# Tail phase: gate products as four column tiles and a summing product, with a new order of work in all queues

## What is computed

```python
x = x + _L0_xattn_ref(_layernorm(x), ctx_1024, ctx_1024, Wq, ... bo)     # softmax attention, 16 heads
x = x + _L0_ffn_ref(_layernorm(x), Wc, bc, W1, b1, W2, b2)               # experts, top token per expert and set
x = x + _L1_xattn_ref(_layernorm(x), ctx_1024, ctx_1024, igate_..., fgate_...)
x = x + _L1_ffn_ref(_layernorm(x), W1, b1, W2, b2)                        # two quantized products with gelu between
```

```python
x = jnp.concatenate([q, k, v], axis=-1)          # q: the normalized x; k and v: the context
ig = x @ igate_kernel + igate_bias               # 1536 -> 8
fg = x @ fgate_kernel + fgate_bias               # 1536 -> 8
```

## Time and profile before

| | us |
|---|---|
| three runs | 2282.11, 2287.96, 2287.25 (median 2287.25) |
| the profiled execution | 2278.25 |
| its span, first to last instruction | 2276.5 |
| the tail, from 1468 us to the end | 808.5 |
| PE busy in the tail | 623.6 |

### The profile page before, as it was taken

How to read it: one execution, slowest core, us unless ns; L and a number is a source line. 1 busy time by engine, 2 the same in 40 slices (tenths; PEclk the granted TensorE clock), 3 DMA queues, 4 the chain that set the end, 5 groups by cost and what they waited for, 6 DMA issues and landing times. The chain is left out here.

```text
span 2276.5 us, 41219 instructions
## 1 busy us (share of the span) xinstructions
PE 1933.3 (85%) x14429; PEld 1218.1 (54%) x14467; DVE 1358.2 (60%) x2542; ACT 1223.8 (54%) x2239; POOL 666.9 (29%) x1205
## 2 busy tenths in 40 slices
PE   6999999999999999998496596336699899889875
PEld 3666666666666666665294294114355455446432
DVE  2757666675767667566233333314687786776763
ACT  2666556565665666555022222244776776676853
POOL 1423321322422231240030130003455345345530
PEclk9999999999999999999697697567898998988988
DMA  6424534243443533341547857686536336324200
GB/s 200 137 81 116 149 98 142 73 130 109 134 129 93 154 80 111 82 114 66 135 142 224 254 151 220 249 335 227 167 102 195 113 102 199 114 96 158 66 19 19
DMA packets 201110, 312.43 MB, mean 137 GB/s; under 512 B 30784, under 2 KB 99488, under 8 KB 193632
## 3 DMA queue, kind: packets, MB, share of 16 engines
q1 hardware_dynamic: 141936, 223.49, 31.2%
q10 hardware_dynamic: 42608, 52.97, 7.4%
q0 software_dynamic: 16384, 33.59, 5.7%
HBM read 171.30 MB, written 71.53 MB: 107 GB/s over the span
## 5 line engine op out<-in xcount | busy, mean ns | idle before, releaser
L506 DVE TENSOR_REDUCE a_negmax<-a_score 128x1 f32<-128x512 f32 x512 | 346.1, 684 | 117.2 <-PE a_score L621 109.0
L441 ACT ACTIVATE a_prob<-a_score,a_negmax 128x512 f32<-128x512 f32 x512 | 353.8, 693 | 94.9 <-DVE a_negmax L506 94.0
L317 POOL DMA_DIRECT2D a_q_stack<-a_q_parts x512 | 250.7, 498 | 520.1 <-DVE a_q_parts L500 254.1
L621 PE MATMUL a_score<-a_k_stack,a_q_stack 128*128 128x512 f32 x512 | 354.3, 692 | 9.6 <-ACT a_prob L441 7.8
L629 PEld LDWEIGHTS a_turn<-a_ident,a_prob 128*128 128x128 f32 x2048 | 254.0, 141 | 134.4 <-issue 93.2
L629 PE MATMUL a_turn<-a_ident,a_prob 128*128 128x128 f32 x2048 | 309.1, 274 | 3.4 <-ACT a_perm L417 2.0
L325 ACT COPY a_probT<-a_turn 128x512 f32<-128x512 f32 x256 | 150.0, 586 | 285.7 <-PE a_turn L629 284.0
L325 DVE COPY a_probT<-a_turn 128x512 f32<-128x512 f32 x256 | 176.3, 689 | 212.9 <-PE a_turn L629 212.6
L1943 PE MATMUL c_ff<-c_w2T,c_hqT 128*128 128x512 bf16 x482 | 140.8, 451 | 40.1 <-ACT c_hqT L1479 34.2
L621 PEld LDWEIGHTS a_score<-a_k_stack,a_q_stack 128*128 128x128 f32 x512 | 97.3, 190 | 112.4 <-issue 75.0
L890 PE MATMUL b_work<-b_blocks,b_xn 128*128 128x256 f32 x512 | 128.5, 417 | 24.7 <-POOL b_blocks L862 24.1
(11 more groups left out here) (206 smaller groups left out, 3326.0 us busy)
## 6 DMA issues: line engine op xcount, KB each, us to landing
a_k_stack<-a_k_parts SPq DMA_DIRECT2D x512, 64.0 KB, 2.6
a_q_stack<-a_q_parts POOLq DMA_DIRECT2D x512, 64.0 KB, 2.3
scratch_res<-b_res SPq DMA_DIRECT2D x32, 1024.0 KB, 5.0
c_res<-scratch_res SPq DMA_DIRECT2D x32, 1024.0 KB, 7.6
b_xn<-scratch_xn SPq DMA_DIRECT2D x68, 256.0 KB, 2.7
c_hid<-in_L_ffn_W ACTq DMA_DIRECT2D x16, 1024.0 KB, 8.4
c_negm<-scratch_m SPq DMA_DIRECT2D x64, 256.0 KB, 4.4
a_xs<-in_x ACTq DMA_DIRECT2D x8, 1024.0 KB, 5.2
```

Source lines behind the costliest of these rows:

```text
L317: eng.dma_start(stack[kind][i * DH0:(i + 1) * DH0, M % 2, g, :].bitcast(F32), parts[kind][g * DH0:(g + 1) * DH0, part, :].bitcast(F32)).th ...
L441: nc.scalar.activation(prob[:, U % 4, :], score.bank(U)[:, :], ACT.Exp, bias=negmax[:, u:u + 1], accum_out=sums[:, head_of(U), tile_of(U): ...
L506: nc.vector.tensor_reduce(negmax[:, U % UNITS:U % UNITS + 1], score.bank(U)[:, :], AX.X, ALU.max, negate=True).then_inc(max_ready, 1)
L621: nc.tensor.matmul(score.bank(U)[:, :], stack["Q"][:, M % 2, g, t * P:(t + 1) * P], stack["K"][:, M % 2, g, :], start=True, stop=True).the ...
```

## The change

The eight gate products of a batch are no longer added up in one bank. A new step GP writes four partial sums beside each other, each in its own 32 columns of the array and its own 32 partitions of one bank: quarter 0 adds products 0 and 1 of gk with xT, quarter 1 products 2 and 3, quarters 2 and 3 do the same for gkv with cT. A new ACT step GC copies the bank (128 x 512, fp32) to gate_parts. The step G is now one product of a constant matrix `picks` (128 x 40) with gate_parts: it adds the four quarters and puts the gates at the rows where they were. The weights lie in 32 columns instead of 40, with the forget gates at 8 to 15. POOL fills picks once, at the start, with a memset and 8 copies. G's bank and what reads it are as before.

All five lists are new. GP stands before DN 1 and G after it. UP 2 and UP 3 stand elsewhere: UP 2 before XT, and UP 3 before SC 0; SC 1 stands after DN 2. Of the later half: ST 1 moves up, SC 2 and SC 3 stand before MIX 0. On SP the second half of the round now reads MOUT, Y 0, GOUT, M 0, GBC 0, Y 1, GBC 1, Y 2, Y 3, X, RES 2, RES 3, M 1, M 2, GBC 2, M 3, RES 0, GBC 3, CT; the first X now comes before RES 2. On POOL: KS 0, KS 1, XG 0, XG 1, MASK 0, MASK 1, KS 2, KS 3, MASK 2, MASK 3, XG 2, XG 3. On ACT: LN 0 after SQ, RH 1 before XTC, and GELU 2 before CH 1.

```diff
-    PE_ORDER = (("UP", 1, -2), ("ST", 1, -1), ("SCO", 1, -1), ("MIX", 0, -1), ("ST", 2, -1), ("SC", 2, 0),
...
+    PE_ORDER = (("HT", 3, -2), ("W", 6, -1), ("ROWS", 0, 0), ("DN", 3, -2), ("W", 1, 0), ("XQ", 0, -1), ("W", 7, -1),
+                ("ST", 0, 0), ("W", 2, 0), ("ST", 1, 0), ("UP", 0, -1), ("UP", 1, -1), ("SCO", 0, 0), ("SC", 2, 1),
+                ("SC", 3, 1), ("TOTAL", 0, 1), ("SCO", 1, 0), ("ST", 2, 0), ("MIX", 0, 0), ("SCO", 2, 0),
+                ("MIX", 1, 0), ("SCO", 3, 0), ("ST", 3, 0), ("MIX", 2, 0), ("HT", 0, -1), ("MIX", 3, 0),
+                ("DN", 0, -1), ("UP", 2, -1), ("W", 3, 0), ("XT", 0, 1), ("HT", 1, -1), ("W", 4, 0), ("GP", 0, 1),
+                ("DN", 1, -1), ("G", 0, 1), ("W", 0, 1), ("W", 5, 0), ("UP", 3, -1), ("SC", 0, 2), ("HT", 2, -1),
+                ("DN", 2, -1), ("SC", 1, 2))
...
+                 ("SQ", 0, 0), ("LN", 0, 1), ("RH", 1, -1), ("WCOPY", 3, 0), ("XTC", 0, 1), ("SUM", 1, 4),
+                 ("SUM", 0, 5), ("QUANT", 0, 1), ("QUANT", 5, 0), ("GELU", 2, -1), ("SUM", 3, 3), ("CH", 1, -1),
+                 ("GC", 0, 1))
...
-        gk, gkv = sb("gk", [P, 3 * C, GM]), sb("gkv", [P, C, GM])
+        gk, gkv = sb("gk", [P, 3 * C, FG]), sb("gkv", [P, C, FG])
+        picks, gate_parts = sb("picks", [P, GM]), sb("gate_parts", [P, S])
...
+                nc.gpsimd.memset(picks[:, :], 0.0).then_inc(picks_ready, 1)
+                pool.wait_ge(picks_ready, 1)
+                pool.wait_ge(const, 2)
+                for j in range(C):
+                    r = slice(j * FG, (j + 1) * FG)
+                    for k in range(2):
+                        nc.gpsimd.tensor_copy(picks[r, k * FG:k * FG + H1], ident[r, j * FG + k * H1:j * FG + (k + 1) * H1]).then_inc(picks_ready, 1)
...
+                def copy_parts(m):
+                    if m > 0:
+                        wait_full(act, "G", m - 1, 0)
+                    j = job["GP", m, 0]
+                    work.wait_full(act, 0, j)
+                    nc.scalar.copy(gate_parts[:, :], work.bank(j)[:, :]).then_inc(work.free[j % 3], 1)
+                    work.wait_read(act, 0, j)
+                    act.sem_inc(parts_ready, 1)
...
-                def gates(m):
-
-                    j = job["G", m, 0]
+                def gate_products(m):
+
+                    j = job["GP", m, 0]
                     pe.wait_ge(xT_ready, (m + 1) * C)
                     pe.wait_ge(cT_in, m * 16 + 16)
                     pe.sem_inc(pe_parted, 1)
                     work.wait_free(pe, 0, j)
                     bank = work.bank(j)
-                    for c in range(C):
-                        nc.tensor.matmul(bank[0:GM, :], gk[:, c, :], xT[:, c, :], start=c == 0, stop=False)
-                    for c in range(C):
-                        last = nc.tensor.matmul(bank[0:GM, :], gkv[:, c, :], cT[:, c, :], start=False, stop=c == C - 1)
+                    for c in range(2):
+                        for q in range(C):
+                            weights, of = (gk, xT) if q < 2 else (gkv, cT)
+                            k = q % 2 * 2 + c
+                            last = nc.tensor.matmul(bank[q * FG:(q + 1) * FG, :], weights[:, k, :], of[:, k, :],
+                                                    start=c == 0, stop=c == 1, skip_group_check=True)
                     last.then_inc(work.full[j % 3], 1)
+
+                def gates(m):
+
+                    j = job["G", m, 0]
+                    pe.wait_ge(parts_ready, m + 1)
+                    work.wait_free(pe, 0, j)
+                    nc.tensor.matmul(work.bank(j)[0:GM, :], picks[:, :], gate_parts[:, :], start=True, stop=True).then_inc(work.full[j % 3], 1)
```

More of the change, by code:

```diff
@@ new lines, in tail_phase @@
+    DVE_ORDER = (("FINISH", 1, -2), ("CLIP", 5, -1), ("EXPAND", 3, -2), ("CLIP", 6, -1), ("SHIFT", 1, -1),
+                 ("ROWS", 0, 0), ("HSCALE", 3, -2), ("CLIP", 1, 0), ("FINISH", 2, -2), ("TOKENS", 0, -1),
+                 ("CLIP", 2, 0), ("COLS", 0, 0), ("CLIP", 7, -1), ("FINISH", 3, -2), ("STATE", 0, 0),
+                 ("STATE", 1, 0), ("EXPAND", 0, -1), ("EXPAND", 1, -1), ("ADD", 0, 1), ("ADD", 1, 1), ("PROD", 0, 0),
+                 ("ADD", 2, 1), ("ADD", 3, 1), ("PROD", 1, 0), ("HSCALE", 0, -1), ("STATE", 2, 0), ("PROD", 2, 0),
+                 ("MOM", 0, 1), ("PROD", 3, 0), ("STATE", 3, 0), ("CLIP", 3, 0), ("HSCALE", 1, -1), ("CLIP", 4, 0),
+                 ("SHIFT", 0, 1), ("NORM", 0, 0), ("WSCALE", 0, 1), ("FINISH", 0, -1), ("EXPAND", 2, -1),
+                 ("SCALE", 0, 0), ("HSCALE", 2, -1), ("X3", 0, 0), ("CLIP", 0, 1))
@@ new lines, in tail_phase @@
+    ACT_ORDER = (("WCOPY", 4, -1), ("RH", 2, -2), ("QUANT", 6, -1), ("LOGS", 0, 0), ("QUANT", 1, 0), ("GELU", 3, -2),
+                 ("CH", 2, -2), ("WCOPY", 0, 0), ("QUANT", 7, -1), ("SUM", 4, 2), ("LN", 1, -1), ("WCOPY", 5, -1),
+                 ("WCOPY", 6, -1), ("LATER", 0, 0), ("LOADW", 0, 10), ("QUANT", 2, 0), ("SUM", 6, 1), ("RH", 3, -2),
+                 ("CH", 3, -2), ("SUM", 7, 1), ("RT", 0, -1), ("SUM", 5, 2), ("WCOPY", 1, 0), ("CTOK", 0, -1),
+                 ("WCOPY", 7, -1), ("DEC", 0, 0), ("GELU", 0, -1), ("DEC", 1, 0), ("WCOPY", 2, 0), ("SUM", 2, 3),
+                 ("GELU", 1, -1), ("QUANT", 3, 0), ("POUT", 0, 0), ("DEC", 2, 0), ("FLOOR", 0, 0), ("POUT", 1, 0),
+                 ("DEC", 3, 0), ("RH", 0, -1), ("QUANT", 4, 0), ("POUT", 2, 0), ("CH", 0, -1), ("POUT", 3, 0),
+                 ("SQ", 0, 0), ("LN", 0, 1), ("RH", 1, -1), ("WCOPY", 3, 0), ("XTC", 0, 1), ("SUM", 1, 4),
+                 ("SUM", 0, 5), ("QUANT", 0, 1), ("QUANT", 5, 0), ("GELU", 2, -1), ("SUM", 3, 3), ("CH", 1, -1),
+                 ("GC", 0, 1))
@@ L1065, in tail_phase @@
+    POOL_ORDER = (("MASK", 0, 0), ("MASK", 1, 0), ("KS", 2, 0), ("KS", 3, 0), ("MASK", 2, 0), ("MASK", 3, 0),
+                  ("XG", 2, 0), ("XG", 3, 0), ("ROOT", 0, 1), ("ADDB", 0, -1), ("HROOT", 0, 0), ("ADDH", 0, 0),
+                  ("ROOT", 1, 0), ("KS", 0, 1), ("KS", 1, 1), ("XG", 0, 1), ("XG", 1, 1))
+    SP_ORDER = (("GBC", 3, -1), ("CT", 0, 0), ("RES", 1, 1), ("PERM", 0, 1), ("V", 0, 0), ("MOUT", 0, 0),
[3 rows of a table added]
     ONCE = ("W", "TOTAL", "SUM", "WSCALE", "QUANT", "CLIP", "WCOPY", "LOADW", "BIAS")
-    BANKS_OF = {"SCO": ("work", 2), "ST": ("work", 1), "XT": ("work", C), "G": ("work", 1), "ROWS": ("work", 1),
+    BANKS_OF = {"SCO": ("work", 2), "ST": ("work", 1), "XT": ("work", C), "GP": ("work", 1), "G": ("work", 1), "ROWS": ("work", 1),
@@ L1969, in _ @@
                         turn_tokens(m)
+                    elif kind == "GP":
+                        gate_products(m)
                     elif kind == "G":
```

7 lines of the change are left out of this document (6 added, 1 removed), and 9 rows, old and new, of tables (PE_ORDER, SP_ORDER).

## The result

The changed kernel takes 2310.82 us in the median (2308.87 to 2318.25), the kernel before 2284.68 in the runs beside it: a ratio of 1.0119, 95% interval 1.0096 to 1.0142. The forecast was 2272 and a gain. The profiled execution has a span of 2307.1 us against 2276.5.

The account below looks back on a forecast made before the run. PE was taken to bound a round, busy 75.2 of 84.05 us. Start -11, six rounds -6 and end +2 took the profiled 2278.25 to 2263.2 us; for the runs' median, 2287.25 - 15 = 2272, range 2248 to 2298.

Parts of the forecast that it names:

- I charge 0.5 us a round, between 0 and 3: Later half, HT 3 to MIX 3: M 1 behind X, RES 2 and RES 3 makes the masks late, 0.5 us a round.
- rival 3: Later half: late M 1 holds up masks and MIX 3, lowering PE's clock; +9 to +20, say 2300 us; chance 0.19.
- charged +0.5: PE's clock in each round: slow stretches at 1.2 GHz move or are added after new waits; +0.5 us, between -2.3 and +3.4.
- a clock under 0.87 in the rounds: PE's clock over the rounds: a sign that would show the forecast wrong and point to rival 2.
- rival 2: First half: second slow stretch at DN 1 in two of three rounds; rounds 1.3 us longer, 2286 us; chance 0.22.
- the 2.1 us: First half of a round: HT 3 starts at +39.1 us after MIX 3, 2.1 us earlier.
- PE bounds a round: Rounds of the tail: PE is what bounds them, busy 75.2 of 84.05 us, with 8.9 us idle.
- The gates: Gate products of each batch: GP 2.0 us and G 0.9 instead of 7.0; PE saves 4.1 us a batch.
- Rival 4: Gate products: the quarters don't run beside each other, +0.9 us a batch, some +12, 2299 us; chance 0.02.
- The start: First two batches: earlier X (some 5.5 us), cheaper gates (3) and earlier GOUT (3); sum -11 us, ends -3 and -18.
- The end: Last batch: GELU 2 before CH 1 delays DN 1 and UP 3; +2 us, ends 0 and +3.
- Rival 1: Rounds: PE's whole saving comes through, a round falls by 3.5 to 4 us; -34, 2253 us; chance 0.15.

Follow-up runs that it names:

- e_ks_early: The changed kernel with KS 2 and KS 3 moved ahead of MASK 1 in POOL's list: 2280.78 us.
- b_m1_first: The changed kernel with M 1 moved ahead of Y 2, Y 3, X, RES 2 and RES 3 in SP's list: 2265.87 us.
- n_sc3_later: The changed kernel with SC 3 moved behind MIX 0, ADD 3 and TOTAL moved with it: 2314.71 us.
- i_two_products: The kernel before with six of the eight gate products left out of every batch (gates then wrong): 2271.02 us.
- h_first_x: The kernel before with only the very first load of x issued right behind the first PERM: 2282.42 us.
- c_order_only: The changed kernel's five new lists with the gates as before, the eight products at G's new place behind DN 1: 2354.83 us.
- a_gates_only: The kernel before with its five old lists and only the gate step new (GP, GC, G): 2292.85 us.

## Why the prediction was wrong

**The later half: the step that failed.** "I charge 0.5 us a round, between 0 and 3": it was +6.6. Its beginning was seen in advance, also as rival 3: M 1 behind X, RES 2 and RES 3, and gaps of PE that lower its clock. POOL's wait comes out at 10 us in the text and was 12.1. Wrong was the path from there, and what it would cost. The text had M 1 land 25 us after HT 3 and the masks end near MIX 3's time, and in rival 3 MIX 3 waits for them. M 1 landed after 22, less late than forecast; the masks ended at 1832.8, 14 us ahead of MIX 3's start, and the sign of rival 3, MIX waiting for masks, did not come. They never were what ended last. What counted was a wait that the text didn't have at all, KS 2 behind MASK 1 in POOL's new list, 1.9 us long. With it gone (e_ks_early) 30 us are back, with M 1 early (b_m1_first) 45: of the 10.5 us a later half, 8.6 are the clock and 1.9 idle time.

**The clock: mis-sized by its place.** I took a stretch at 1.2 GHz as 7 us long wherever it falls, because the earlier trace rows and its neighbours showed that, and charged +0.5. The text doesn't have the stretch in front of MIX 3 and DN 0, which the trace of before shows in every round, though the DN 0 of the earlier trace rows, 5.42 us long, lies in it. Ahead of the MIX steps a stretch lasted 10, 14, 27, 27 and 31 us in the five rounds, and 10 to 14 in n_sc3_later. The sign to watch, "a clock under 0.87 in the rounds", came: 0.84 in the 456.2 us from the second MIX 3 to the seventh, against 0.90 in the same stretch of the kernel before. The text had it as the sign of rival 2, a stretch at DN 1; most of it lies in the later half.

**The first half: right in the single steps, wrong in what bounds it.** In the changed kernel's round from 1757.31 the steps stand almost where I had put them:

```profile
1769.37 0.62 PE L1879 MATMUL c_work<-c_xT,c_gk 128*32 128x512 f32 x2 [0.15 <-ACTq L1442]
...
1774.98 4.79 PE L1975 MATMUL c_ff<-c_w2T,c_hqT 128*128 128x512 bf16 x15 [3.68 <-ACT c_hqT L1498]
...
1779.69 1.05 PE L1888 MATMUL c_work<-c_gate_parts,c_picks 128*40 128x512 f32 x2
...
1791.18 5.08 PE L1975 MATMUL c_ff<-c_w2T,c_hqT 128*128 128x512 bf16 x15 [3.93 <-ACT c_hqT L1498]
```

GP at +12.1 (forecast +12.1), DN 1's wait 3.68 us (3.3), DN 2's wait 3.93 (3.7). DN 1 then ran at the low clock, 4.79 instead of 3.4 us, HT 3 came at +40.8 instead of +39.1, and the 2.1 us were gone: rival 2's term, as described. But the sentence "PE bounds a round" was wrong for this half: i_two_products takes 5.2 us from PE and the half stays at 40.9 us (before 40.6). Forecast were halves 2 us shorter; in the mean they are 0.6 longer. The busy shares of the earlier trace rows are means over both halves. The waits of the earlier trace rows, for ACT, with DVE's 7 us of gate rows behind them, had said so, and the text read them so and then still let half of PE's saving through.

**The gates.** GP 1.7 to 1.8 and G 1.0 us against 2.0 and 0.9: right, 4.3 us of PE saved a batch. Rival 4 is excluded.

**The start.** -12.5 measured, -11 forecast, but by wrong terms: the early X gives 2.5 us (h_first_x), not 5.5. c_order_only, with the new lists and old gates, needs 202.4 us to the second MIX 3, against 203.4 before and 191.0 in the changed kernel, so most of it came with the new gates, but only in the new lists: a_gates_only needs 203.3. By which of its waits was not tested. That the forecast start nearly fits is luck.

**The end.** +3.6 measured against +2, not tested.

**The rivals' sums.** Rival 1 leaves out the +2 of the end, which the forecast has, and rival 3 takes -8 for the start where the forecast has -11, without a reason.

**The sum.** Forecast -11 - 6 + 2 = -15. Measured -12.5 + 3.8 + 33.0 + 3.6 = +27.9, and +2.7 in the phases that the change doesn't touch. The 33.0 are the miss: the forecast has the later half 0.5 us longer a round, and 0.5 more for the clock.
